# A conditioned linear-attention layer: TensorE's loop widened to turns 2 to 15, work reordered in the first turns and in the tail

## The reference

```python
xn = _ln(x, ln_w, ln_b)
q = xn @ Wq + bq
k = xn @ Wk + bk + (1.0 - src_mask) * -1000000.0
q = softmax(q.reshape(b, t, h, dh), axis=-1)
k = softmax(k.reshape(b, t, h, dh), axis=1)
v = ((xn @ Wv + bv) * src_mask).reshape(b, t, h, dh)
att = einsum('bnhd,bnhl->bhdl', k, v)
y = einsum('bnhd,bhdl->bnhl', q, att).reshape(b, t, d)
emb_out = (silu(emb) @ W_emb + b_emb)[:, None, :]
scale, shift = split(emb_out, 2, axis=2)
hh = _ln(y, ln2_w, ln2_b) * (1.0 + scale) + shift
return x + silu(hh) @ W_out + b_out
```

## Time and profile before

| | us |
|---|---|
| median of 3 runs | 306.88 |
| lowest, highest | 306.3, 309.34 |
| the profiled execution's own time | 307.7 |
| its span, first to last instruction | 305.8 |

### The profile page before, as it was taken

The page is one execution under the profiler, slowest core; times in us unless marked ns, Lnnn a source line. Parts: engine busy times, 40 slices in busy tenths (PEclk is TensorE's granted clock), DMA queues, the critical chain, the costliest instruction groups (busy, mean ns, idle before and its releaser), DMA issues.

```text
span 305.8 us, 14375 instructions
## 1 busy us (share of the span) xinstructions
PE 291.8 (95%) x5528; PEld 248.5 (81%) x5528; DVE 272.4 (89%) x640; ACT 237.0 (77%) x592; POOL 244.6 (80%) x246
## 2 busy tenths in 40 slices
PE   7999789899999999999999999999999999989875
PEld 7578588788989888988889898889888898877655
DVE  5899999989999999999999999999999796967793
ACT  1567758787978988898979888888989798776443
POOL 2275748989998989999998989898999979873470
PEclk9999999999999999999999999999999999999999
DMA  6983430704527080815325180906251341002024
GB/s 198 315 298 109 129 115 5 236 10 117 198 66 248 1 308 1 253 56 176 133 106 203 46 263 1 298 11 231 78 169 71 90 150 53 17 4 72 4 71 137
DMA packets 28445, 38.61 MB, mean 126 GB/s; under 512 B 2433, under 2 KB 20481, under 8 KB 28418
## 3 DMA queue, kind: packets, MB, share of 16 engines
q1 hardware_dynamic: 28000, 37.94, 38.1%
q10 hardware_dynamic: 418, 0.30, 0.3%
HBM read 29.80 MB, written 8.45 MB: 125 GB/s over the span
## 4 chain that ended last, share of the span: by engine, by line
PE 82%; DVE 9%; issue 4%; POOL 2%; DMA 1%; POOLq 1%; ACT 0%; SPq 0%; DVEq 0%
PE bk L1113 27%; PE bv L1113 27%; PE by L1113 15%; PE by L1198 4%; PE by L1177 4%; PE bv L1189 4%; DVE xstat L785 2%; DMA x_all<-in_x 1%; DVE k_t L909 1%; DVE q_s L898 1%; POOLq L45 1%; DVE qmax L890 1%; DVE th L843 1%; POOL xr L485 1%; DVE ystat L986 0%
## 5 line engine op out<-in xcount | busy, mean ns | idle before, releaser
L641 ACT ACTIVATE k_t<-k_t,kmax 128x64 f32<-128x64 f32 x240 | 60.5, 336 | 6.4 <-DVE kmax L916 6.2
L476 POOL TENSOR_TENSOR x_all<-x_all,bo_all 128x1024 f32 (+1 forms) x16 | 40.1, 2508 | 0.2
L436 POOL TENSOR_TENSOR h_lo<-h_s,h_hi 128x512 fp32r<-128x512 f32 x30 | 38.3, 1297 | 0.9 <-ACT h_hi L660 0.8
L445 POOL TENSOR_TENSOR xt_raw<-xt_raw,rows 128x512 f32<-128x512 f32 x28 | 37.0, 1322 | 1.5 <-DMA rows<-rows_dram 1.5
L447 POOL TENSOR_TENSOR xt_raw<-xt_raw,rows 128x512 f32<-128x512 f32 x28 | 36.5, 1303 | 2.2
L286 POOL TENSOR_TENSOR z_s<-z_s,mod_shift 128x512 f32<-128x512 f32 x30 | 30.7, 1044 | 6.8 <-DVE z_s L930 6.8
L595 ACT ACTIVATE y_s<-y_s,yr 128x256 f32<-128x256 f32 x56 | 29.1, 593 | 3.8 <-POOL yr L468 3.8
L1113 PE MATMUL bv<-w_o_hi,h_hi 128*128 128x256 f32 x120 | 31.6, 285 | 0.0
L1113 PE MATMUL bv<-w_o_lo,h_hi 128*128 128x256 f32 x120 | 31.0, 280 | 0.0
L580 ACT ACTIVATE v_s<-bk,small 128x256 f32<-128x256 f32 x32 | 15.1, 474 | 17.7 <-PE bk L1113 16.4
L1113 PEld LDWEIGHTS by<-kv,q_t 32*64 32x64 f32 x2048 | 22.4, 130 | 6.9 <-issue 6.5
(11 more groups left out here) (163 smaller groups left out, 865.9 us busy)
## 6 DMA issues: line engine op xcount, KB each, us to landing
x_all<-in_x SPq DMA_DIRECT2D x15, 512.0 KB, 6.4
out<-x_all SPq DMA_DIRECT2D x15, 512.0 KB, 5.0
xt_raw<-in_x_t SPq DMA_DIRECT2D x14, 512.0 KB, 6.1
rows<-rows_dram SPq DMA_DIRECT2D x14, 512.0 KB, 4.2
off<-in_mask_rows SPq DMA_DIRECT2D x16, 256.0 KB, 6.1
rows_dram<-xr_rows SPq DMA_DIRECT2D x56, 1.0 KB
x_all<-in_x SPq DMA_DIRECT2D x2, 256.0 KB, 3.5
z_s<-in_w_emb SPq DMA_DIRECT2D x1, 512.0 KB, 7.2
```

Of the source, the lines that this page charges most:

```text
L436: nc.gpsimd.tensor_tensor(h_lo[:, c, :], h_s[:, c, :], h_hi[:, c, :].bitcast(fp32), ALU.subtract).then_inc(hlo_d, 1)
L445: nc.gpsimd.tensor_tensor(xc, xc, rows[:, parity, 0, :], ALU.mult).then_inc(xm_d, 1)
L476: nc.gpsimd.tensor_tensor(xg, xg, bo_all[:, :].unsqueeze(1).broadcast_to([P, T, D]), ALU.add).then_inc(xb_d, 1)
L641: last = nc.scalar.activation(kk, kk, ACT.Exp, scale=-1.0, bias=kmax[:, c, n:n + 1])
```

## The change

- PE: turns 0 and 1 are unrolled, turns 2 to 15 are a loop of 7 passes of two turns, then the tail. Turn 2 takes the order of K's products that the loop has. Group 13's output products are in turn 15, no longer in the tail. `res_d` starts at 2, by ACT's first instruction, so that the loop's waits are on positive values.
- The table: `emb_products` write `bt[1]`; the wait of `exp_k_transposed(1)` on `emb_out` is gone.
- W_out: ACT makes `w_o_hi` in turn 0 with scale 0.5 (`weights_o_high`, after `v_tile(0,0,0)`), DVE makes `w_o_lo` in one operation (`weights_o_low`).
- Turn 0: POOL normalizes tiles 2 and 3 of group 1 (ACT had all four); POOL does `x_biased(0)` before `x_rstd(2)`; ACT exchanges `k_exp_first(0)` and `v_tile(0,0,2)`; DVE interleaves `q_max`, `q_shifted` and the statistics of group 2 and does `x_rows(2)` last, after `x_stats(3,1)`.
- Turn 1: DVE does `y_scaled_all(0)` before `q_shifted(1,1,0)`.
- Tail: h of group 14 is rounded into the space of `w_qv_hi` and `w_qv_lo`, its first half before group 15's `y_hat` (ACT) and `y_rstd` (POOL); DVE does `residual(13,1)` and `h_product(M,0)` before `y_sums(L)`.

```diff
+        h_hi_m = w_qv_hi
+        h_lo_m = w_qv_lo
...
-        def steps(eng, body, tail, after_first=None, loops=G // 2 - 3):
+        def steps(eng, body, tail, after_first=None):
...
             def store(g):
-                wait(sp, res_d, 2 * g + 2)
+                wait(sp, res_d, res_base + 2 * g + 2)
...
                     x_rstd(1)
+                    pool.wait_ge(xt_d, 2)
+                    pool.wait_ge(xr_d, 8)
+                    for t in (2, 3):
+                        nc.gpsimd.tensor_scalar(xhat[:, t, :], x_all[:, 1, t * D:t * D + D], xr[:, 0, t:t + 1],
+                                                xr[:, 1, t:t + 1], ALU.mult, ALU.add).then_inc(xhat_d, 1)
                     return
...
                     k_shifted(0)
                     k_shifted(1)
+                    x_biased(0)
                     x_rstd(2)
...
-                if not last_turn(i):
-                    x_biased(i)
                 if first(i):
                     x_rstd(3)
+                elif not last_turn(i):
+                    x_biased(i)
...
+            def late_low(c):
+
+                pool.wait_ge(hhi_d, 2 * M + c + 1)
+                nc.gpsimd.tensor_tensor(h_lo_m[:, c, :], h_s[:, c, :], h_hi_m[:, c, :].bitcast(fp32),
+                                        ALU.subtract).then_inc(hlo_d, 1)
+
             def tail():
                 shifts(M)
+                late_low(0)
                 y_rstd(0)
                 y_half_hat(0)
                 y_rstd(1)
                 y_half_hat(1)
-                h_low(M, 0)
-                h_low(M, 1)
+                late_low(1)
...
-            nc.scalar.activation(yr[:, 1, :], neg_half[:, :], ACT.Tanh)
+            nc.scalar.activation(yr[:, 1, :], neg_half[:, :], ACT.Tanh).then_inc(res_d, res_base)
...
+            def weights_o_high():
+
+                act.wait_ge(wo_in, 16)
+                nc.scalar.activation(w_o_hi[:, :, :], w_o, ACT.Copy, scale=0.5).then_inc(wo_high, 1)
...
-                for t in range(T):
+                for t in (0, 1):
                     nc.scalar.activation(xhat[:, t, :], x_all[:, 1, t * D:t * D + D], ACT.Identity,
...
                     v_tile(0, 0, 0)
+                    weights_o_high()
                     v_tile(0, 0, 1)
                     x_hat_one()
+                    v_tile(0, 0, 2)
                     k_exp_first(0)
-                    v_tile(0, 0, 2)
                     v_tile(0, 0, 3)
...
+            def late_high(c):
+
+                act.wait_ge(qv_d, 4 * L + 4)
+                act.wait_ge(h_d, 2 * M + c + 1)
+                nc.scalar.activation(h_hi_m[:, c, :], h_s[:, c, :], ACT.Copy).then_inc(hhi_d, 1)
...
                 z_tanh(M, th_of)
+                late_high(0)
                 act.wait_ge(yr_d, 2 * L + 2)
                 y_hat(0)
-                h_high(M, 0)
-                h_high(M, 1)
+                late_high(1)
...
-            def weights_o():
-
-                dve.wait_ge(wo_in, 16)
-                link(nc.vector.tensor_scalar(w_o, w_o, 0.5, None, ALU.mult))
-                split(w_o, w_o_hi, w_o_lo)
+            def weights_o_low():
+
+                dve.wait_ge(wo_high, 1)
+                nc.vector.scalar_tensor_tensor(w_o_lo[:, :, :], w_o, 0.5, w_o_hi[:, :, :].bitcast(fp32),
+                                               ALU.mult, ALU.subtract).then_inc(weights_ready, 1)
...
                 if first(i):
-                    x_stats(2, 0)
-                elif not (isinstance(i, int) and i + 2 >= G):
+                    q_max(0, 0)
+                    q_shifted(0, 0, 0)
+                    x_variances(2, 0, (0, 1, 2))
+                    q_max(0, 1)
+                    q_shifted(0, 0, 1)
+                    x_variances(2, 0, (3,))
+                    x_means(2)
+                    x_low(1, by[:, 2:4, :])
+                    x_stats(3, 1)
+                    x_rows(2)
+                    return
...
                 if second(i):
-                    weights_o()
+                    weights_o_low()
                     silu_cond()
...
-                if B:
-                    y_sums(i - 1)
-                q_shifted(i, par, 0)
-                if B:
+                y_sums(i - 1)
+                if second(i):
+                    y_scaled_all(0)
+                    q_shifted(1, 1, 0)
+                else:
+                    q_shifted(i, par, 0)
                     y_scaled_all(i - 1)
...
             def tail():
+                residual(L - 2, 0)
                 kv_scaled(L)
-                residual(L - 2, 0)
                 z_scaled(M)
+                residual(L - 2, 1)
+                h_product(M, 0, th_of)
                 y_sums(L)
                 y_scaled(L, 0)
                 y_stats(L, (0, 1))
                 y_scaled(L, 1)
                 y_stats(L, (2, 3))
-                h_product(M, 0, th_of)
                 h_product(M, 1, th_of)
                 half_z(0)
-                residual(L - 2, 1)
...
-                        last = mm(be[1][:, j * BATCH:(j + 1) * BATCH], w_e[c // 2][:, c % 2, j * P:(j + 1) * P],
+                        last = mm(bt[1][:, j * BATCH:(j + 1) * BATCH], w_e[c // 2][:, c % 2, j * P:(j + 1) * P],
...
                 for e in range(2):
-                    if second(g) and e == 1:
-                        pe.wait_ge(emb_out, 2 * C)
...
-                if isinstance(i, int) and i <= 2:
+                if isinstance(i, int):
...
-                if O and not last_turn(i):
-                    if isinstance(i, int) and i == 2:
-                        pe.wait_ge(weights_ready, 3)
+                if second(i):
+                    pe.wait_ge(weights_ready, 3)
+                if O:
...
             def tail():
                 exp_k_transposed(L, 0)
-                pe.wait_ge(qsub_d, 4 * L + 1)
-                out_product(L - 2, 0)
                 attention(L, 1)
                 q_transposed(L, 1)
                 y_transposed(M)
                 y_product(L)
-                pe.wait_ge(qsub_d, 4 * L + 2)
-                out_product(L - 2, 1)
...
-                pe.wait_ge(res_d, 2 * (L - 2) + 1)
+                pe.wait_ge(res_d, res_base + 2 * (L - 2) + 2)
                 x_added(M, 0, bv_)
+                x_added(M, 1, bv_)
                 half_y_transposed(1)
-                pe.wait_ge(res_d, 2 * (L - 2) + 2)
-                x_added(M, 1, bv_)
-                out_product(M, 0)
-                out_product(M, 1)
+                late_out(0)
+                late_out(1)
...
-            steps(pe, body, tail, loops=G // 2 - 2)
+            body(0, 0, True, True, False, False, True)
+            body(1, 1, True, True, True, False, True)
+            with pe.Fori(1, G // 2) as turn:
+                body(2 * turn, 0, True, True, True, True, True)
+                body(2 * turn + 1, 1, True, True, True, True, True)
+            tail()
```

40 lines of the change are left out of this document (23 added, 17 removed).

## The result

The changed kernel takes 308.66 us (median of 22 runs, 307.56 to 310.16); the kernel before, on the same chips, 309.04 us (22 runs, 306.3 to 311.67). The ratio of the two is 1.0045, 95% interval 1.0024 to 1.0066. So the change gains nothing and most likely loses 0.5%; 304.0 us was forecast, and 308.66 lies outside the range given.

The account below looks back on a forecast made before the run. PE, busy throughout the loop, was taken as the bound, so only the first turns, turn 15 and the tail could give. Gains of 2.0 and 0.9, together 2.9 us, off the median 306.88 gave 304.0 us, range 302.3 to 306.0.

Parts of the forecast that it names:

- W_out, 3.8 us saved, 1.7 at the least: First turns, DVE: one operation instead of three, 0.7 us or at most 1.78, and a shorter silu_cond, save 3.8 us.
- The table's bank, at most 1.1 us: First turns, PE: the 0.8 us wait for the table and the pipeline's restart go, 1.1 us at most.
- Turn 0: 1.6 us on k of group 1, 4.3 on the rows of group 2: Turn 0: the new order delays k of group 1 by 1.6 us and group 2's rows by 4.3 us.
- Group 2's rows: transpose to landed took 6.5: First turns: the rows, transposed at 27.75 us, land 6.5 us later, at 34.2, as the kernel before took.
- Gain of the first turns: 2.0: First turns: turn 2's attention starts at 46.2 instead of 48.29 us, gain 2.0, between 0.9 and 2.8.
- The clock: Whole kernel: PE taken at its full 2.4 GHz level, 1.00 in every stretch used.
- Turn 15 in the loop, 1.8 us: Turn 15, PE: 18.64 us with its output products becomes 16.86, as issue gaps and their restarts go, 1.8 us.
- y_sums(L) 0.5 us late for a gain later: Tail, DVE: y_sums(L) starts 0.5 us late behind tanh; the last copy then starts at 301.5, not 302.50.
- The first turns give only half: Rival, chance 0.18: group 2's rows still later or POOL slowed in x_scaled; gain 0.9 + 0.9, 305.1 us.
- The tail gives nothing: Rival, chance 0.11: attention behind the loop stalls about 1 us for instructions; gain 2.0 or less, 305.0 us.
- Both ends give their upper bound: Rival, chance 0.21: rows land faster and y_sums is not held; 2.7 + 1.7 = 4.4, giving 302.5 us.
- the only one on the slower side: Rival, chance 0.08: PE's loop no longer stays in the instruction store; 6 returns at 3 us, 18, giving 322 us.

Follow-up runs that it names:

- e7: Kernel before with ACT making w_o_hi, DVE's single w_o_lo, table in bt[1] without its wait, y_scaled_all(0) ahead of q_shifted: 303.39 us, ratio 0.9839 to before.
- e12: Kernel before with only ACT's w_o_hi and DVE's single-operation w_o_lo, the table's bank and DVE's order unchanged: 305.25 us, ratio 0.9931 to before.
- e1: Changed kernel with DVE doing x_rows(2) before x_stats(3,1) in turn 0: 308.05 us, ratio 1.0007 to the kernel before.
- e11: e7 with the whole new order of turn 0 put in: 305.08 us, ratio 0.9961 to the kernel before.
- e2: Changed kernel with five useless filling products on PE in the tail, ahead of half_y_transposed(0): 306.83 us, ratio 0.9969 to the kernel before.
- e14: Changed kernel with two useless filling products on PE in turn 1, ahead of y_product(0): 310.22 us, ratio 1.0034 to the kernel before.
- e3: Changed kernel with the edits of e1 and e2 together: 306.14 us, ratio 0.9954 to the kernel before.
- e4: e2 with turn 0 of POOL, ACT and DVE in the old order: 305.74 us, ratio 0.9938 to the kernel before.
- e9: e4 with K's high products before its low ones in every turn, three fills with group 14's x instead of five: 309.64 us, ratio 1.015 to before.
- e10: e7 once more, unchanged, on another chip: 303.84 us, ratio 0.9926 to the kernel before.
- e8: Kernel before with two useless filling products on PE in the tail, ahead of half_y_transposed(0): 309.97 us, ratio 1.0049 to the kernel before.
- e13: e7 with the changed kernel's tail for h of group 14, PE's loop and group 13's products as before: 304.29 us, ratio 0.9838 to before.
- e6: Kernel before with PE's loop over turns 2 to 15, res_d from 2 and the table in the other bank: 310.81 us, ratio 1.0057 to before.

## Why the prediction was wrong, point by point

- **PE's time in the loop can't be bettered, only the ends give.** Right: turns 2 to 14 differ by 0.02 us.
- **W_out, 3.8 us saved, 1.7 at the least.** Right in kind and, in the changed kernel, in size: 0.68 and 0.68 at 33.43 and 34.03. With e7's and e12's rows both bounds of the new operation have been seen (0.68 and 1.80). The Trainium skill's "GPSIMD Engine Reference", section 1, Specifications, has it that GpSimd shares SBUF interfaces with VectorE instructions of two SBUF inputs; the rows of e12 agree, and e7's silu beside POOL's `xt_raw` again took 1.78. The 0.68 of e7's `w_o_lo`, begun just ahead of POOL's operation, shows that overlap alone does not lengthen the VectorE one.
- **The table's bank, at most 1.1 us.** Right: from the table's first product to turn 2's attention it is 9.08 us in e7 (35.74 to 44.82) and 10.17 in e12 (36.70 to 46.87), 1.1 less with the other bank. The remaining 0.4 between them goes with DVE's order, costed at 0.6 of DVE's time.
- **Turn 0: 1.6 us on k of group 1, 4.3 on the rows of group 2.** The delays were right (PE's wait for q_t of 0.7 was 0.81 in e1 and 0.87 in e11; transpose at 28.00). The step that failed is the next one, **"Group 2's rows: transpose to landed took 6.5"**. It was followed only forward, to POOL. Backward, the buffer `xr_rows` is free only when the four stores are done, and `x_rows(3)` stands behind it in DVE's stream: 1.57 us there, 1.80 for PE's y product. And the 6.5 was no constant: 36.15 - 28.00 = 8.15, and 7.8 in e2, 6.75 in e1, 6.25 in e11. From the transpose to the issue of the load it was 4.3 us in this execution, 2.7 in before's.
- **"Gain of the first turns: 2.0", bounds 0.9 and 2.8.** Measured 0 in the profiled execution, 0.6 where the clock stays up (e2 and e14). The 0.9 bound had rows 1 us late and no clock. What the weights, the bank and DVE's order in turn 1 bring is 3.2 us (e7); the changed kernel hands all of it back. Taken away one after the other, the losses in the head are: the clock's fall 0.5 (20.83 to 20.28, e2), the late rows 1.4 (to 18.85, e3), the rest of turn 0's new order 0.45 (to 18.40, e4), the loop's order of K in turn 2 0.8 (to 17.61, e9, and e7 has 17.62). In another order the shares would differ, as these stand beside each other. The last one was put at nothing: the change gives turn 2 the loop's order, and the sum has no term for it. The sign of being wrong that the text named, a wait on xt_lo in turn 2's K over 0.5 us, came in e2 (0.81), e14 (0.55) and e4 (0.52).
- **The clock.** The text took 1.00 for every stretch because every stretch of the trace of before had it. It priced idle time of PE at its length, in both directions. The second step that failed is that the cover of the products of group 13 was costed for attention(15) alone; that much was right (PE waited 0.74 for e_k). That half of them also lay ahead of PE's wait for group 15, which becomes 4.52 us, does not stand in the prediction at all, nor does any price for it. e2 measured it: 1.9 us.
- **Turn 15 in the loop, 1.8 us.** The mechanism was right: there is no issue gap, and from attention 14 to 15 it takes 13.15 us with all 24 products, before 12.63 with 12 of them. But part of what leaves turn 15 comes back as PE's wait in the tail. The size was one execution's. In kernels with turn 15 unrolled, attention 14 to 15 took 12.63, 12.60, 12.03, 12.44, 12.87, 12.82 and 12.49 us (before, e7, e10, e12, e11, e8, e13): it varies by 0.8 us with the gaps.
- **y_sums(L) 0.5 us late for a gain later.** The lateness was right (DVE waited 0.62 us for tanh; e13 has `y_sums(L)` 0.6 later than e7), the gain later was not: e13 is 0.9 slower by its profile. At the full clock turn 15 and the tail together gain 0.1 us (e2) and not 0.9. The chain from `y_sums(L)` to PE's first half is the one that ends last; h of group 14 was needed only behind it.
- **The rivals.** "The first turns give only half" had the right place, the late rows, but not the wait of the next writer, K's order or the clock. "The tail gives nothing" came out by another mechanism (its issue stall never came: no gap in attention 15). "Both ends give their upper bound" adds 2.7 and 1.7 where the text's own upper bound for the first turns is 2.8. The loop does stay in the instruction store: 11 packets on q8 in the whole span, one of them, at 112 us, behind the loop's first pass and none from there to 284 us. None of the rivals contained the clock, and none put PE's idle time in the tail in the place of the removed work; the only one on the slower side had 0.08 and did not happen.

Open: what decides, in executions with nearly the same wait, whether the clock falls. Ahead of the falls stood waits of 1.80 (after), 2.49 (e13), 2.8 (e8), 3.3 (e6), 3.7 (e1), 4.0 (e14) and 4.5 us (after); waits of 1.47 (e2), 1.88 (e7), 1.97 (before) and 2.9 us (e6's first turns) had none behind them. Open too: why group 2's four stores were slow in the changed kernel, e2 and e14 (DVE waited 1.57, 1.23 and 1.43 us) and not in e11, which has the same order of turn 0.

## What to carry to other kernels

On an engine that is busy 95% of the time, work that lies in front of a wait is cover, not cost: before moving it away, look at how long the wait becomes, and at the granted clock on both sides of the few waits that there are. When a step is delayed, follow its buffer backward as well as its result forward: the next writer of the same buffer may stand in the stream of the engine that you meant to relieve. And try a change of many parts part by part: here one part alone is faster by 1.6% in one set and by 0.7% in another (there against before's executions at the full clock), and the rest of the change costs that and more.
